# Key and value projection of the last stage as three fp32r products of split operands

## The reference, cut to what matters

```python
x = _layernorm(x + _L0_attn_ref(x, Wq, Wk, Wv, Wo))
x = _layernorm(x + _L0_xattn_ref(ctx, ctx, x, ssm_kernel, D, 8))
x = _layernorm(x + _L0_ffn_ref(x, W_gate, W_qkv))
# in the last one:
gating = softmax(x @ W_gate.T); idx = argmax(gating)
q, k, v = split(x @ W_qkv.T, 3)
k_shared = the 16 key values of head idx of each token
v_shared = top gate value * the 16 value features of head idx
y = causal softmax attention of the 16 query heads over k_shared, v_shared
```

## Time and profile before

| | us |
|---|---|
| median of 3 runs | 363.72 (361.96 to 364.12) |
| the profiled execution, its time | 363.41 |
| its span (first to last instruction) | 361.6 |
| PE busy | 317.1 (88%) |
| DVE busy | 260.7 (72%) |
| ACT busy | 217.8 (60%) |
| POOL busy | 201.2 (56%) |

### The profile page before, as it was taken

How to read it: one execution, slowest core, us unless ns; L and a number is a source line. 1 busy time by engine, 2 the same in 40 slices (tenths; PEclk the granted TensorE clock), 3 DMA queues, 4 the chain that set the end, 5 groups by cost and what they waited for, 6 DMA issues and landing times.

```text
span 361.6 us, 6079 instructions
## 1 busy us (share of the span) xinstructions
PE 317.1 (88%) x2016; PEld 237.7 (66%) x2016; DVE 260.7 (72%) x497; ACT 217.8 (60%) x663; POOL 201.2 (56%) x283
## 2 busy tenths in 40 slices
PE   1948799999999999999999999777298999999972
PEld 0745688788788788778778768554054666566541
DVE  2774975964984874885874875978759889998543
ACT  3638557657647747747747646513147777777781
POOL 0487643756663765671774672577657369832112
PEclk9979999999999999999999999989779999999998
DMA  7911000031010022000012000000000000000001
GB/s 255 367 47 58 3 30 2 1 111 65 1 31 0 2 73 102 3 29 2 0 44 84 2 2 0 3 0 0 0 2 2 2 0 16 17 16 16 0 16 44
DMA packets 5614, 13.06 MB, mean 36 GB/s; under 512 B 848, under 2 KB 3024, under 8 KB 5328
## 3 DMA queue, kind: packets, MB, share of 16 engines
q1 hardware_dynamic: 5040, 11.90, 9.6%
q10 hardware_dynamic: 544, 0.79, 0.7%
HBM read 11.63 MB, written 1.05 MB: 35 GB/s over the span
## 4 chain that ended last, share of the span: by engine, by line
PE 71%; DVE 15%; issue 5%; POOL 3%; DMA 2%; ACT 2%; SPq 1%; POOLq 0%; DVEq 0%; ACTq 0%
PE bank L465 12%; PE bank L344 12%; PE bank L375 8%; PE bank L361 7%; PE bank L454 6%; PE bank L572 4%; PE bank L606 4%; PE bank L617 4%; PE bank L443 4%; DVE toep L985 3%; PE bank L627 2%; DMA anti<-in_anti 2%; PE bank L601 2%; DVE t_cos L950 2%; PE bank L563 1%
## 5 line engine op out<-in xcount | busy, mean ns | idle before, releaser
L1339 POOL TENSOR_TENSOR prob<-prob,rden 128x512 f32<-128x512 f32 x32 | 33.5, 1045 | 72.5 <-DVE rden L1012 72.5
L1318 POOL TENSOR_TENSOR t_sin<-rot,sin 128x512 f32<-128x512 f32 x40 | 54.2, 1357 | 26.4 <-ACT rot L736 23.6
L760 ACT ACTIVATE prob<-bank,neg_max 128x128 f32<-128x128 f32 x128 | 45.3, 367 | 39.2 <-DVE neg_max L1005 39.1
L344 PE MATMUL bank<-x_hi,w_hi 128*128 128x512 f32 x96 | 36.9, 466 | 8.5 <-ACT w_hi L717 8.0
L375 PEld LDWEIGHTS bank<-k_rope,q_rope 128*128 128x128 f32 x256 | 35.0, 200 | 10.5 <-DVE q_rope L963 5.1
L465 PE MATMUL bank<-wo_hi,head_hi 128*128 128x256 f32 x128 | 39.1, 306 | 3.0 <-DVE head_lo L1039 3.0
L883 ACT ACTIVATE prob<-bank,fneg_max 128x128 f32<-128x128 f32 x128 | 36.7, 378 | 6.5 <-DVE fneg_max L1227 6.5
L375 PE MATMUL bank<-k_rope,q_rope 128*128 128x128 f32 x256 | 35.6, 284 | 4.7 <-DVE q_rope L963 4.7
L465 PE MATMUL bank<-wo_lo,head_hi 128*128 128x256 f32 x128 | 36.4, 284 | 0.0
L465 PE MATMUL bank<-wo_hi,head_lo 128*128 128x256 f32 x128 | 36.3, 284 | 0.0
L1397 POOL TENSOR_TENSOR rstd<-var_eps,half_pow 128x1 f32<-128x1 f32 (+1 forms) x18 | 10.8, 601 | 45.7 <-DVE var_eps L1158 44.7
(11 more groups left out here) (103 smaller groups left out, 738.8 us busy)
## 6 DMA issues: line engine op xcount, KB each, us to landing
w_raw<-in_wqkv SPq DMA_DIRECT2D x3, 768.0 KB, 5.8
toep<-in_toep SPq DMA_DIRECT2D x8, 256.0 KB, 3.0
wo_raw<-in_wo SPq DMA_DIRECT2D x4, 512.0 KB, 3.5
x_raw<-in_xt SPq DMA_DIRECT2D x2, 512.0 KB, 5.8
ctxT<-in_ctx SPq DMA_DIRECT2D x1, 1024.0 KB, 9.2
x<-in_x SPq DMA_DIRECT2D x1, 1024.0 KB, 9.8
out<-x SPq DMA_DIRECT2D x8, 128.0 KB, 1.7
wf<-in_wf SPq DMA_DIRECT2D x1, 784.0 KB, 4.4
```

The source lines that it names most:

```text
L344: last = pe.matmul(out[:, :], wp[:, c, col:col + P], xp[:, j, c, :], start=(c + n == 0), stop=(c == C - 1 and n == 2))
L760: last = act.activation(prob[:, k % 2, h * P:(h + 1) * P], score_bank[k % 2][:, h * P:(h + 1) * P], ACT.Exp, bias=neg_max[:, k % 2, h:h + ...
L1318: pool.tensor_tensor(t_sin[:, par, :].rearrange("p (b t) -> p b t", b=BH), rot[:, par, :].rearrange("p (b t) -> p b t", b=BH), sin[:, :].u ...
L1339: pool.tensor_tensor(own, own, rden[:, k % 2, :].unsqueeze(2).to_broadcast([P, HG, P]), ALU.mult).then_inc(norm_done, 1)
```

## The change

`wf_hi` and `wf_lo` (key and value columns of the weights, split as above) and `x2_hi` and `x2_lo` (the transposed state of a block, split) are kept in the room of `x_hi` and `x_lo`, which phase A no longer needs. `kv_project` issues for each half three fp32r matmuls in place of one fp32 matmul. ACT gets one cast of the weights in the last unit and a cast of `mix_bank` after every `x2_copy`; DVE gets one subtraction for the weights and, for every block, `x2_low`, a subtraction that reads `mix_bank`. In DVE's stream `x2_low(i+1)` stands behind `mix_sum(i+2)` and ahead of `gating(i+1)`. On PE, `x1_turn` waits for `x2_low` where it waited for `x2_copy`, and the first half of `kv_project(b)` waits for `x2_low(b)` and for the split weights. `gate_project` and `query_project` stay in fp32 on `x2T`.

```diff
--- before.py
+++ after.py
@@ -121,6 +121,9 @@
 
         kblock = w_raw[:, :, D:2 * D]
         wf = sb("wf", [P, C, 3 * D + FH])
+        wf_hi, wf_lo = x_hi[:, 0, :, :], x_lo[:, 0, :, :]
+        x2_hi = x_hi[:, 1, 0, :].rearrange("p (j d) -> p j d", d=D)
+        x2_lo = x_lo[:, 1, 0, :].rearrange("p (j d) -> p j d", d=D)
         qmix = rot[:, :, 0:D]
         mixT = t_cos[:, :, 0:D]
         x2T = k_rope[:, :, 0:D]
@@ -208,6 +211,10 @@
         mix_done = sem("mix_done")
         x2T_done = sem("x2T_done")
         x2copy_done = sem("x2copy_done")
+        x2hi_done = sem("x2hi_done")
+        x2lo_done = sem("x2lo_done")
+        wf_hi_done = sem("wf_hi_done")
+        wf_lo_done = sem("wf_lo_done")
         gate_mm_done = sem("gate_mm_done")
         gate_done = sem("gate_done")
         kvf_done = sem("kvf_done")
@@ -532,7 +539,7 @@
                 if b in (1, 3):
                     pe.wait_ge(qmix_done, b)
                 elif b:
-                    pe.wait_ge(x2copy_done, max(1, b - 2))
+                    pe.wait_ge(x2lo_done, max(1, b - 2))
                 for c in range(C):
                     last = pe.transpose(mix_bank[:, c * P:(c + 1) * P], x[:, b, c * P:(c + 1) * P],
                                         ident[:, :])
@@ -569,8 +576,11 @@
                 if c == 0:
                     at_least(pe, masked_done, b, 1)
                     at_least(pe, ynorm_done, b, 3)
-                last = pe.matmul(kvf_bank[:, :], x2T[:, j, c * P:(c + 1) * P], wf[:, c, D:3 * D],
-                                 start=(c == 0), stop=(c == C - 1))
+                    pe.wait_ge(x2lo_done, b + 1)
+                    pe.wait_ge(wf_lo_done, 1)
+                for n, (xp, wp) in enumerate(((x2_hi, wf_hi), (x2_hi, wf_lo), (x2_lo, wf_hi))):
+                    last = pe.matmul(kvf_bank[:, :], xp[:, j, c * P:(c + 1) * P], wp[:, c, :],
+                                     start=(c + n == 0), stop=(c == C - 1 and n == 2))
                 if c == C - 1:
                     last.then_inc(kvf_done, 1)
 
@@ -809,6 +819,8 @@
                     exps(u, 3)
                     head_copy(1)
                     mix_query(1, 1)
+                    act.wait_ge(in_ffn, 48)
+                    act.copy(wf_hi[:, :, :], wf[:, :, D:3 * D]).then_inc(wf_hi_done, 1)
                     head_copy(2)
                     head_copy(3)
                     return
@@ -848,6 +860,7 @@
             def x2_copy(b, j):
                 act.wait_ge(x2T_done, b + 1)
                 act.copy(x2T[:, j, :], mix_bank[:, 0:D]).then_inc(x2copy_done, 1)
+                act.copy(x2_hi[:, j, :], mix_bank[:, 0:D]).then_inc(x2hi_done, 1)
 
             def gate_copy(b):
                 act.wait_ge(gate_mm_done, b + 1)
@@ -1069,6 +1082,7 @@
                     prob_copy(2)
                     dve.wait_ge(near_done, 1)
                     mix_sum(0, 0)
+                    split_lo(wf_lo[:, :, :], wf[:, :, D:3 * D], wf_hi[:, :, :], wf_hi_done, 1, wf_lo_done)
                     prob_copy(3)
                     head_low(2)
                     add_mix(0, 0)
@@ -1083,6 +1097,7 @@
                     second_apply(0, 0)
                     first_apply(2, 0)
                     head_low(3)
+                    x2_low(0, 0)
                     gating(0)
                     accumulate(1)
                     return
@@ -1185,6 +1200,11 @@
                 norm_eps(0, ln2, b)
                 second_apply(b, j)
 
+            def x2_low(b, j):
+                dve.wait_ge(x2hi_done, b + 1)
+                dve.tensor_tensor(x2_lo[:, j, :], mix_bank[:, 0:D], x2_hi[:, j, :].bitcast(FP32),
+                                  ALU.subtract).then_inc(x2lo_done, 1)
+
             def gating(b):
                 dve.wait_ge(gate_done, b + 1)
                 at_least(dve, gexp_done, b, 1)
@@ -1273,6 +1293,7 @@
                 if 2 <= i + 2 < NB:
                     mix_sum(i + 2, i % 2)
                 if 1 <= i + 1 < NB:
+                    x2_low(i + 1, (i + 1) % 2)
                     gating(i + 1)
                 if 0 <= i < NB:
                     frow_max(i, 2)
```

## The result

The changed kernel takes 390.7 us (median of 4 runs, 388.8 to 391.9) against 362.8 us before (median of 4): slower, ratio 1.076, 95% interval 1.070 to 1.0825. The forecast was 376.5 us with a range of 372.5 to 382. The direction and the wait were right, the size was not: +27.9 us where the forecast had added some 13 (11.3 for the wait and the matmuls, 1.7 for the clock).

The account below looks back on a forecast made before the run. PE was taken to set the pace, busy all of a block's 11.46 us, with DVE 0.4 us from full. Waits 13.1 + 0.75, less 2.6 for matmuls, gave +11.3; 374.8 plus a 1.7 us clock spell made 376.5, range 372.5 to 382.

Parts of the forecast that it names:

- The wait: PE waits for x2_low at x1_turn or kv_project: 2.08, 2.08, 2.83, 2.76, 2.76, 0.58 us in blocks 2 to 7, 13.1 together.
- case 5: Not slower: DVE finishes mix_sum early in later blocks, so only the first 2.1 us wait and 0.75 are paid; 363.7, chance 0.05.
- That the wait passes in full into the time: Blocks 2 to 7: PE and DVE work in turn, so all 13.1 us count; a block lasts 14.1 against 11.6 us.
- the sum without clock: Whole kernel: 13.1 + 0.75 - 2.6 = +11.3 us, before any loss from half clock.
- The matmuls: kv_project's six fp32r matmuls take 1.39 us against 1.72, saving 0.33 us a block, 2.6 us in all, bounds 0 and 2.6.
- Splits at nothing: Last unit: ACT's weight cast (1.05 us) and DVE's subtraction (1.40 us in a 1.89 us gap) are free.
- The clock: The new long waits in the blocks bring one spell of half clock, 1.7 us, taking 374.8 to 376.5.
- Case 3: The wait, with the clock down after most waits: five spells of 1.7 us, 8.5 on 374.8; 378.5 to 385, chance 0.15.

Follow-up runs that it names:

- filling: The changed kernel with 8, 8, 11, 11 and 11 more fp32r matmuls on PE in its five long waits; 377.4 us, ratio to before 1.041.
- The products alone: The kernel before with kv_project's six fp32r products but no splits or waits for them, so its results are not the reference's; 362.1 us, ratio 0.9957.

## Why the prediction was wrong, point by point

**The wait: right.** Place, releaser and all six lengths came out within 0.06 us, from rows of the kernel before alone. So did the loop: DVE's 8.79 us from share on didn't shrink, and case 5 (DVE runs ahead) didn't happen.

**That the wait passes in full into the time: right, nearly.** With the clock kept up by filling the loss is 14.6 us, against 11.3 in the sum without clock (it came to 374.7 or 375.0 us by its two bases, and 374.8 was carried on, which changes nothing); in its profile 12.5 of them lie between share(1) and share(7), where the sum has 13.1 less six times 0.33, that is 11.1. That profile has the distances between shares at 14.2, 13.6, 14.4 and 13.8 us for blocks 1 to 5, where "about 13.5 to 14.2 us" was said. What is over lies in block 1 (2.2 us), in the smaller saving of the next point, and for the rest in the filling itself or unexplained.

**The matmuls: rather too high.** Six products do take 1.39 us (249.54 to 250.95 in the changed kernel), as read from phase A. But where nobody waits for the split, 0.33 us saved on PE a block became 0.25 us of time (67.5 against 69.0 over six blocks), with x2_low's 0.41 us on a DVE that is nearly full in it. The products alone gave 1.1 to 1.6 us, with an interval up to the 2.6 that the sum took; so the term was within 1.5 us of right, and no trace shows where the rest went.

**Splits at nothing: slightly off.** The weights' subtraction took 1.68 us, not 1.40:

```profile
L987 DVE TENSOR_TENSOR x_lo<-wf,x_hi 128x1024 fp32r<-128x1024 f32 x1 | 1.7, 1682 | 0.0
```

It was costed against a gap of 1.89 us which itself existed because PE ran at half clock just there. In the changed profile the clock fell some 5 us later, PE was done earlier, and prob_copy(3) came right behind the subtraction, at 240.71, with PE idle for 2.36 us. A cover read from one trace was a cover under one course of the clock. All splits together, without anybody waiting for them, cost 0.6 to 1.3 us.

**The clock: the term that failed.** The step that failed is the last term of the sum: one spell of half clock at 1.7 us. Five spells (8.5 us) had a chance of 0.15. The runs show 13.3 us. Two things were wrong in it. The count: four of the five long waits brought a spell. And the length: the price was read from one spell of 3.5 us, while in the changed kernel the four lasted 10.2, 3.4, 10.2 and 6.8 us. The spell goes on while PE works: from the release of PE to share it took 8.8, 5.0, 6.5, 8.5 and 7.3 us in blocks 2 to 6, against 5.2, 5.2, 5.2, 5.2 and 5.1 before, which is 10.0 us more, and 11.7 with the 0.33 that the products save each time. The trace of before had shown a long spell as well: block 1 stayed at half clock from 257.2 to 267.5 us, 5 us beyond PE's resumption, which the prediction didn't price. The section HAM oscillation of the page TensorE: Matmul & The Clock Gate in the Trainium skill describes a loop that falls back in every round, there in waits for a DMA, and the trace agrees with it more than with the forecast: four of five, in waits of 2.0 to 2.8 us for DVE. I had cited it and then set the count by the rows, at one. Case 3 had the right mechanism and, at 385 us, too small a price.

## What to carry to other kernels

Before an instruction is put behind another on a busy engine, look at what is waiting on the other side: 0.41 us of work behind a reduction of 2.27 us cost 28 us, and moved in front of it 4. A wait on TensorE that comes back in every block is to be priced twice, once for itself and once for the clock it may bring down: here, with waits of 2.0 to 2.8 us, the second was as large as the first (13.3 and 13.1 us), and waits of 1.70 us brought the clock down too. A cover found in one trace should be asked whether it would be there if the clock ran otherwise.

## What the runs showed of the hardware

Once down, the granted clock stayed at 0.50 for 3.4 to 17 us, also while PE was busy 89% of the time (279.5 to 289.5 us in the changed kernel, with transposes, score matmuls and kv_project); how long isn't explained by these runs. Idle times of 1.70 us twice went with a fall, others of 1.73 and 2.05 us did not. Feeding PE throwaway matmuls during a wait gave back 13.3 us of 390.7, and half as many gave back 12.0. Between executions of one unchanged kernel the mean granted clock and the time go together (before, medians over 64 executions: 361.8 us at 0.978, 363.1 at 0.973, 363.5 at 0.969, 364.2 at 0.965), so much of its scatter of 361.4 to 365.8 us may be where the spells of half clock fall; that isn't shown, since only one of them has a trace. And a granted clock of 1.00 doesn't say that PE runs at its usual pace: in one execution of 624.4 us the hi x hi matmuls of phase A took 817 ns in place of 466.
